# Order of TensorE's three kinds of attention products inside one core step of a two-layer macaron block

## Chip, cores and metric

The program runs on one core of a Trainium2 chip. The metric is the device time of one execution in microseconds (us), the median of several runs.

## The reference

The input is 8 sequences of 1024 tokens with 256 features. Six residual sublayers follow each other, each on a layernorm of the residual: a gated feed-forward block, linear attention (16 heads, chunks of 64), the gated block again, a routed low-rank layer, causal softmax attention, and the routed layer again. The softmax attention is what the change touches:

```
q = q * cos + rotate_half(q) * sin
k = k * cos + rotate_half(k) * sin
scores = jnp.einsum('bhqd,bhkd->bhqk', q, k) * scale
scores = jnp.where(causal, -jnp.inf, scores)
attn = jax.nn.softmax(scores, axis=-1)
out = jnp.einsum('bhqk,bhkd->bhqd', attn, v)
```

The kernel takes it over 1024 tokens and 16 heads of 16 features for each of the 8 sequences.

## The kernel before

**Three streams.** The work of each engine is a list of pieces, one list for each *tick* of a fixed plan (`weave`). The *front* generators bring a sequence (two halves of 512 tokens, `c` = 0 and 1) through the first sublayers up to rotated q and k, which go to DRAM. The *core* is the softmax attention, in steps; the *tail* generators do the output product and the last sublayer. Fronts and tails of other sequences run in the same ticks as the core, and fill the engines beside it. Within a tick the order is: part 0 of the core step, front `c` = 0, part 1, front `c` = 1, part 2, tails. A table (`STEPS`) says how many core steps a tick has, mostly one.

**The core.** A group is 4 heads of one sequence; there are 32 groups. A group takes two passes.

- *First pass*: `score(g, i)` multiplies q by k for a 128-query block (one to two matmuls, up to 512 columns in all) into one of two PSUM banks. VectorE takes the row maximum of each (line 1115 for blocks with the causal diagonal, line 1118 for the others), and adds 1 to the semaphore `r_used` when it has read a bank. The two banks are a ring, `r_take`: product number n waits until number n-2 has been read. Two kinds of transposes go through the same ring: that of the maxima (line 818, one a group) and that of the sums of values (line 812, two a group). VectorE runs its core pieces one tick later than TensorE.
- *Second pass*: `tscore(u)` multiplies k by q, for one key block and two heads: two matmuls of 128 to 512 columns, into banks 0 and 1. ScalarE takes the exponential of each (line 1321). There is one bank for each of the two heads, so the product for unit u, half j, waits until the exponential of unit u-1, half j, has been read (`exp_done`). GpSimd zeroes what lies above the diagonal (line 1469).
- *Values*: `values(u)`, every second step, multiplies four heads' exponentials by v (line 795); it waits for the exponentials and for GpSimd.

A core step t has the transposed products of unit u+1 (u = t - 129) in part 0, the values in part 1 when u is even, and up to three first-pass products of the group that is 30 steps ahead, one in each part, as the table `USES` says: mostly one in a step with values and two in a step without. A sequence has 96 steps and 144 first-pass products.

A semaphore wait stands in TensorE's own queue, and matmuls leave it in the order of the program. The lines that the change reorders are in `core_pe`.

Of the kernel before, what the change touches and what calls it, by code (L numbers as in the profile page):

```python
# [18 lines left out]
NB = B  # L19
# [37 lines left out]
def macaron(nc, a, out):  # L57
    ctx = ExitStack()
    with ctx:
# [105 lines left out]
        def ps(i, n=1):  # L165
            return bank[i // 2][:, (i % 2) * CH:(i % 2) * CH + n * CH]
# [213 lines left out]
        NU = NTU * NG  # L380
# [14 lines left out]
        score_at = {}  # L395
# [18 lines left out]
        def width(c, kb):  # L414
            return CH - max(0, kb - 4 * c) * P

        def slot(g, hp):
            return (2 * g + hp) % NSLOT

        def loads(g, hp):  # L420

            return (2 * g + hp) // NSLOT + 1
# [11 lines left out]
        if True:  # L434

            with nc.Block() as block:
# [22 lines left out]
                def r_take(*key):  # L459
                    n = len(rtab)  # L460
                    rtab[key] = n
                    if n >= 2:
                        nc.tensor.wait_ge(s["r_used"], n - 1)
                    return ps(3 + n % 2)
# [289 lines left out]
                def score(g, i):  # L754

                    h, blocks = sunits[i]
                    b_ = slot(g, h // 2)
                    nc.tensor.wait_ge(stack_in[b_], 16 * ND * loads(g, h // 2))
                    bk = r_take("s", g, i)
                    for qb, k0, n, col in blocks:  # L760
                        last = mm(bk[:, col:col + n], stq[b_][:, h % 2, qb * P:(qb + 1) * P], stk[b_][:, h % 2, k0:k0 + n],  # L761
                                  start=True, stop=True)
                    last.then_inc(s["r_full"], 1)

                def tscore(u):

                    g, i = divmod(u, NTU)
                    c, kb, hp = tunits[i]
                    if i == 0:
                        nc.tensor.wait_ge(max_in[g % 2], 64 * (g // 2 + 1))  # L770
                    n = width(c, kb)
                    b_ = slot(g, hp)
                    for j in range(2):
                        if u >= 1:
                            nc.tensor.wait_ge(s["exp_done"], 2 * u + j - 1)
                        mm(ps(j)[:, 0:n], stk[b_][:, j, kb * P:(kb + 1) * P],  # L776
                                  stq[b_][:, j, (c + 1) * CH - n:(c + 1) * CH], start=True, stop=True).then_inc(
                                      s["t_ps"], 1)

                def values(u):  # L780

                    g, i = divmod(u, NTU)
                    c, kb, _ = tunits[i]
                    yu = NC * g + c
                    n = width(c, kb)
                    if g % NG == 0 and kb % 4 == 0:
                        nc.tensor.wait_ge(s["v_in"], 32 * (g // NG) + 16 * (kb // 4 + 1))
                    nc.tensor.wait_ge(s["exp_done"], 2 * u + 2)
                    if i in DIAG:
                        nc.tensor.wait_ge(s["causal"], len(DIAG) * g + DIAG.index(i) + 1)  # L790
                    if kb == 0 and yu >= 1:
                        nc.tensor.wait_ge(s["ypv_done"], yu)
                    for j in range(G):
                        at = VP * (G * (g % NG) + j)
                        last = mm(ps(2)[HP * j:HP * (j + 1), CH - n:CH], vsm[:, kb, at:at + HP], pexp[:, (u - 1 + j // 2) % NPX, j % 2, 0:n],  # L795
                                  start=kb == 0, stop=kb == 4 * c + 3, tile_position=(0, HP * j))
                    last.then_inc(s["pv_done"], 1)

                def core_pe(t, part):
                    u = t - SX  # L800
                    if part == 0 and 0 <= u + 1 < NU * NB:
                        tscore(u + 1)
                    if part == 1 and u % 2 == 0 and 2 <= u < NU * NB + 1:
                        values(u - 1)
                    if (t, part) in score_at:
                        score(*score_at[t, part])
                    if part == 2 and t in y_tr_at:
                        g, c = y_tr_at[t]
                        nc.tensor.wait_ge(s["ypv_done"], NC * g + c + 1)
                        bk = r_take("y", g, c)  # L810
                        for k in range(4):
                            last = nc.tensor.transpose(bk[:, k * P:(k + 1) * P], ypv[:, c, k * P:(k + 1) * P], ident[:])
                        last.then_inc(s["r_full"], 1)
                    if part == 2 and t in max_tr_at:
                        g = max_tr_at[t]
                        nc.tensor.wait_ge(s["mx_comb"], g + 1)
                        bk = r_take("m", g)
                        nc.tensor.transpose(bk[0:G * NT, 0:P], mxa[:, g % 2], ident[:]).then_inc(s["r_full"], 1)

                @block.tensor  # L820
                def _(pe):
                    weave(core_pe, front_pe, tail_pe)
# [792 lines left out]
```

## Time and profile before

| | |
|---|---|
| median of 3 runs | 2871.23 us (2869.66 to 2884.01) |
| profiled execution, its own time | 2874.38 us |
| its span, first to last instruction | 2872.6 us |
| TensorE (PE) | 2595.6 us busy, 90% |
| VectorE (DVE) | 1856.1 us, 65% |
| ScalarE (ACT) | 1227.1 us, 43% |
| GpSimd (POOL) | 746.5 us, 26% |

Busy time is the union of the records of an engine. A matmul's record reaches from its start to the end of its pipeline, so that records of matmuls that follow each other overlap. PEld are the weight loads of TensorE.

### The profile page before, as it was taken

Reading aid. Unit: us, or ns where it says so; the run is one execution under the profiler, and the core shown is the slowest. Engines: PE = TensorE matmul, PEld = TensorE weight load, DVE = VectorE, ACT = ScalarE, POOL = GpSimd, SP = SyncE. Lnnn points to the kernel's source line nnn. Section 1 sums busy time; section 2 is a strip of 40 time slices with the busy share of each in tenths; the row PEclk is TensorE's granted clock in tenths of the full one; section 3 lists DMA queues with packets and bytes.
Section 4 is the critical chain, followed back from the end, with each engine's and each line's share of the span. In section 5 each row is a group of like instructions: output and inputs, shape, how many; then the busy total and the mean of one; then the engine's idle time right before and its main releaser. Section 6 shows DMA issues by size and latency. Waiting matters only on the chain.

```text
span 2872.6 us, 45484 instructions
## 1 busy us (share of the span) xinstructions
PE 2595.6 (90%) x15278; PEld 1723.4 (60%) x15278; DVE 1856.1 (65%) x5534; ACT 1227.1 (43%) x2802; POOL 746.5 (26%) x1283
## 2 busy tenths in 40 slices
PE   3885899989999999999999999999999999998996
PEld 3563566556666666566655666566665666555644
DVE  5543667766677667776677766676677766776642
ACT  1321244455444444444444444444444444444452
POOL 2322222223322232223322232222322233221111
PEclk7987899999899999999999999999999999999997
DMA  2014112321244112322044112341124221343311
GB/s 61 1 45 120 22 41 62 109 60 40 48 108 110 40 42 62 116 71 65 18 113 125 42 34 61 95 110 40 42 62 131 63 58 30 97 123 74 75 36 48
DMA packets 137423, 193.97 MB, mean 68 GB/s; under 512 B 49439, under 2 KB 111214, under 8 KB 127854
## 3 DMA queue, kind: packets, MB, share of 16 engines
q1 hardware_dynamic: 131808, 190.89, 26.3%
q8 instruction: 129, 2.11, 0.3%
q10 hardware_dynamic: 5390, 0.18, 0.1%
q14 instruction: 96, 0.79, 0.1%
HBM read 122.34 MB, written 67.63 MB: 66 GB/s over the span
## 4 chain that ended last, share of the span: by engine, by line
PE 69%; DVE 16%; DMA 8%; issue 2%; POOL 2%; ACT 1%; SPq 1%; DVEq 0%; ACTq 0%; POOLq 0%
PE bank L776 9%; PE bank L795 8%; PE bank L761 8%; DMA arena<-rope_table 6%; PE bank L598 5%; PE bank L578 4%; PE bank L547 4%; PE bank L529 4%; DVE bank L1115 4%; PE bank L538 3%; PE bank L689 3%; PE bank L703 3%; PE bank L633 2%; PE bank L508 2%; PE bank L572 2%
## 5 line engine op out<-in xcount | busy, mean ns | idle before, releaser
L1321 ACT ACTIVATE pexp<-bank 128x512 f32<-128x512 f32 (+3 forms) x1536 | 677.3, 498 | 571.6 <-PE bank L776 571.1
L1115 DVE CUSTOM_DVE_ANT_0 bank<-bank,maskneg 128x256 f32<-128x256 f32 (+3 forms) x1024 | 484.7, 511 | 266.0 <-PE bank L761 262.0
L776 PE MATMUL bank<-stq,stk 128*128 128x512 f32 (+3 forms) x1536 | 548.6, 427 | 28.9 <-ACT pexp L1321 23.6
L761 PE MATMUL bank<-stk,stq 128*128 128x512 f32 (+3 forms) x1536 | 505.3, 393 | 68.3 <-DVE mxa L1115 24.0
L776 PEld LDWEIGHTS bank<-stq,stk 128*128 128x128 f32 x1536 | 267.9, 195 | 315.4 <-ACT pexp L1321 190.5
L1118 DVE TENSOR_REDUCE mxa<-bank 128x1 f32<-128x512 f32 x512 | 346.3, 684 | 144.7 <-PE bank L761 140.3
L1469 POOL TENSOR_SCALAR_AFFINE_SELECT pexp<-pexp 128x256 f32<-128x256 f32 x512 | 213.2, 424 | 753.7 <-ACT pexp L1321 753.6
L761 PEld LDWEIGHTS bank<-stk,stq 128*128 128x128 f32 x1536 | 281.2, 197 | 180.6 <-issue 142.0
L795 PE MATMUL bank<-pexp,vsm 128*32 128x512 f32 (+3 forms) x3072 | 342.4, 519 | 20.1 <-POOL pexp L1469 19.9
L1387 POOL TENSOR_SCALAR_AFFINE_SELECT arena<-arena 128x512 f32<-128x512 f32 x128 | 78.6, 639 | 404.4 <-ACT arena L1223 404.4
L598 PE MATMUL bank<-arena 32*128 32x256 f32 x1024 | 153.7, 419 | 8.0 <-DVE arena L922 5.0
L508 PE MATMUL bank<-ident,arena 128*128 128x128 f32 x768 | 117.0, 300 | 47.0 <-DVE arena L839 42.3
L922 DVE TENSOR_TENSOR arena<-bank,mask 128x512 f32<-128x512 f32 x128 | 82.4, 685 | 92.6 <-PE bank L598 92.6
L529 PE MATMUL bank<-arena,wk 128*128 128x256 f32 x512 | 137.2, 419 | 4.7 <-DVE arena L863 4.5
L508 PEld LDWEIGHTS bank<-ident,arena 128*128 128x128 f32 x768 | 100.0, 156 | 65.7 <-DVE arena L839 47.9
L795 PEld LDWEIGHTS bank<-pexp,vsm 128*32 128x32 f32 x3072 | 62.6, 110 | 123.4 <-issue 95.2
L1140 ACT COPY xnT<-bank 128x512 f32<-128x512 f32 x160 | 88.3, 601 | 107.5 <-PE bank L508 107.2
L1338 POOL TENSOR_SCALAR varep<-mv 128x4 f32<-128x4 f32 x96 | 22.6, 235 | 417.6 <-DVE mv L833 417.1
L598 PEld LDWEIGHTS bank<-arena 32*128 32x128 f32 x1024 | 92.5, 194 | 57.2 <-issue 39.9
L529 PEld LDWEIGHTS bank<-arena,wk 128*128 128x128 f32 x512 | 107.8, 214 | 28.9 <-issue 6.1
L538 PE MATMUL bank<-wr,arena 128*128 128x256 f32 x512 | 122.9, 383 | 0.1
L839 DVE TENSOR_SCALAR arena<-x,mv,rstd 128x256 f32<-128x256 f32 x320 | 114.8, 420 | 12.0 <-POOL rstd L1340 11.3
(186 smaller groups left out, 4058.4 us busy)
## 6 DMA issues: line engine op xcount, KB each, us to landing
stq<-q_halves SPq DMA_DIRECT2D x128, 256.0 KB
arena<-rope_table SPq DMA_DIRECT2D x8, 2048.0 KB
q_halves<-arena SPq DMA_DIRECT2D x32, 512.0 KB, 2.8
k_halves<-arena SPq DMA_DIRECT2D x32, 512.0 KB, 2.9
stk<-k_halves SPq DMA_DIRECT2D x64, 256.0 KB
stk<-k_halves SPq DMA_DIRECT2D x128, 128.0 KB
v_rows<-arena SPq DMA_DIRECT2D x16, 544.0 KB, 4.1
vsm<-v_rows SPq DMA_DIRECT2D x16, 544.0 KB, 3.7
```

What stands on the lines that cost most here:

```text
L508: last = nc.tensor.transpose(bk[:, t * P:(t + 1) * P], src[:, t, k * P:(k + 1) * P], ident[:])
L529: last = mm(bk[:, m * D:(m + 1) * D], wk0[:, k, m * P:(m + 1) * P], xmA[:, h, k], start=k == 0, stop=k == KT - 1)
L538: last = mm(bk[:, i * D:(i + 1) * D], xmB[:, p, k, i * P:(i + 1) * P], wr0[:, k], start=k == 0, stop=k == KT - 1)
L547: last = mm(bk[:, i * D:(i + 1) * D], kact[:, p, k, i * P:(i + 1) * P], wv0[:, k], start=k == 0, stop=k == KT - 1)
L598: last = mm(bks[i][:, k * D:(k + 1) * D], khT[rows, k, j * P:(j + 1) * P], qbd[rows, j % 2, k], start=k == 0, stop=k == KT - 1, skip_group ...
L761: last = mm(bk[:, col:col + n], stq[b_][:, h % 2, qb * P:(qb + 1) * P], stk[b_][:, h % 2, k0:k0 + n], start=True, stop=True)
L776: mm(ps(j)[:, 0:n], stk[b_][:, j, kb * P:(kb + 1) * P], stq[b_][:, j, (c + 1) * CH - n:(c + 1) * CH], start=True, stop=True).then_inc(s["t ...
L795: last = mm(ps(2)[HP * j:HP * (j + 1), CH - n:CH], vsm[:, kb, at:at + HP], pexp[:, (u - 1 + j // 2) % NPX, j % 2, 0:n], start=kb == 0, sto ...
L1115: last = nc.vector.tensor_tensor_reduce(out=sc, in0=sc, in1=maskneg[:, CH - n:CH], scale=1.0, scalar=LOWEST, op0=ALU.add, op1=ALU.max, acc ...
L1118: last = nc.vector.reduce_max(dst, sc, AX)
L1321: nc.scalar.activation(pexp[:, u % NPX, j, 0:n], ps(j)[:, 0:n], ACT.Exp, scale=DK ** -0.5).then_inc(s["exp_done"], 1)
L1469: nc.gpsimd.affine_select(out=v, in_=v, compare_op=ALU.is_ge, fill=0.0, base=0, pattern=[[0, 2], [1, P]], channel_multiplier=-1).then_inc( ...
```

## The change

In each core step's part 0 the first-pass product, if there is one, now stands ahead of the transposed products; in part 1 it stands ahead of the values. In part 2 nothing changes, nor on any other engine. The front and tail pieces stand where they stood, between the parts.

```diff
                 def core_pe(t, part):
                     u = t - SX
+                    if (t, part) in score_at:
+                        score(*score_at[t, part])
+                    if part == 1 and u % 2 == 0 and 2 <= u < NU * NB + 1:
+                        values(u - 1)
                     if part == 0 and 0 <= u + 1 < NU * NB:
                         tscore(u + 1)
-                    if part == 1 and u % 2 == 0 and 2 <= u < NU * NB + 1:
-                        values(u - 1)
-                    if (t, part) in score_at:
-                        score(*score_at[t, part])
                     if part == 2 and t in y_tr_at:
```

TensorE's queue at units 434 and 435, before. Line 776 is `tscore`, line 761 `score`, line 795 `values`; in brackets stand the semaphores that the instruction waits for (`stack` is the load of q and k).

```order
L776 MATMUL bank<-stq,stk 128x384 [waits exp_done] x2
L761 MATMUL bank<-stk,stq 128x512 [waits r_used,stack3]
L761 MATMUL bank<-stk,stq 128x256 [waits r_used,stack3]
L761 MATMUL bank<-stk,stq 128x256
L776 MATMUL bank<-stq,stk 128x384 [waits exp_done] x2
L761 MATMUL bank<-stk,stq 128x512 [waits r_used,stack3]
L795 MATMUL bank<-pexp,vsm 32x512 [waits ypv_done,causal,exp_done]
L795 MATMUL bank<-pexp,vsm 32x512 x3
```

The same place after the change, from the transposed products of unit 434 on.

```order
L776 MATMUL bank<-stq,stk 128x384 [waits exp_done] x2
L761 MATMUL bank<-stk,stq 128x256 [waits r_used,stack3]
L761 MATMUL bank<-stk,stq 128x256
L761 MATMUL bank<-stk,stq 128x512 [waits r_used,stack3]
L776 MATMUL bank<-stq,stk 128x384 [waits exp_done] x2
L795 MATMUL bank<-pexp,vsm 32x512 [waits ypv_done,causal,exp_done]
L795 MATMUL bank<-pexp,vsm 32x512 x3
```

The 512-column first-pass product of the second step has changed places with the pair of transposed products that was ahead of it. (The one of the first step has done so too; it now stands above the rows shown.)

TensorE's queue at unit 395, before:

```order
L776 MATMUL bank<-stq,stk 128x512 [waits exp_done] x2
L761 MATMUL bank<-stk,stq 128x512 [waits r_used,stack0]
L795 MATMUL bank<-pexp,vsm 32x512 [waits ypv_done,exp_done,v_in]
L795 MATMUL bank<-pexp,vsm 32x512 x3
L598 MATMUL bank<-arena 128x256 [waits f_free2,qbd1,f_free0,f_free1]
```

and after:

```order
L761 MATMUL bank<-stk,stq 128x512 [waits r_used,stack0] x2
L776 MATMUL bank<-stq,stk 128x512 [waits exp_done] x2
L795 MATMUL bank<-pexp,vsm 32x512 [waits ypv_done,exp_done,v_in]
L795 MATMUL bank<-pexp,vsm 32x512 x3
L598 MATMUL bank<-arena 128x256 [waits f_free2,qbd1,f_free0,f_free1]
```

The first of the two merged rows on line 761 is the second product of the step before; the other has moved ahead of the transposed pair. The values and the front's product (line 598) stand where they did.

## Rows read from the trace of the kernel before

**Rows 1.** The page: span, TensorE's busy time, granted clock in 40 slices.

```profile
span 2872.6 us, 45484 instructions
PE 2595.6 (90%) x15278; PEld 1723.4 (60%) x15278; DVE 1856.1 (65%) x5534; ACT 1227.1 (43%) x2802; POOL 746.5 (26%) x1283
PEclk7987899999899999999999999999999999999997
```

**Rows 2.** Busy time in the stretch where the core runs beside fronts.

```profile
core 0: us, PE busy (x) PEld busy (x) DVE busy (x) ACT busy (x) POOL busy (x), PEclk, DMA share, GB/s
370.00:2500.00 2130.00, 2018.04 (x12207) 1344.39 (x12206) 1449.04 (x4346) 974.97 (x2234) 582.72 (x998) 0.97 0.28 69
```

**Rows 3.** Waits, whole span: who waited for whom: us, times, longest.

```profile
ACT pexp L1321 <- PE bank L776: 571.1, 433, 6.5
...
DVE bank L1115 <- PE bank L761: 262.0, 219, 7.5
...
DVE mxa L1118 <- PE bank L761: 140.3, 115, 3.8
```

**Rows 4.** TensorE's own waits, whole span, same columns.

```profile
PE bank L761 <- DVE mxa L1115: 24.0, 28, 3.1
PE bank L776 <- ACT pexp L1321: 23.6, 35, 1.3
...
PE bank L761 <- DVE mxb L1115: 23.5, 40, 1.7
...
PE bank L818 <- DVE mxa L1115: 18.9, 17, 1.3
...
PE bank L761 <- DVE mxa L1118: 11.1, 20, 1.0
...
PE bank L812 <- DVE mxb L1115: 7.1, 9, 1.3
...
PE bank L812 <- DVE mxa L1118: 4.3, 5, 1.8
```

**Rows 5.** Timeline, TensorE, nothing waited for: start us, us, what.

```profile
1499.88 0.63 PE L776 MATMUL bank<-stq,stk 128*128 128x512 f32 x2
1500.35 0.40 PE L761 MATMUL bank<-stk,stq 128*128 128x512 f32 x1
1500.68 0.64 PE L795 MATMUL bank<-pexp,vsm 128*32 128x512 f32 x4
```

**Rows 6.** Timeline at units 434 and 435; in brackets idle before, releaser.

```profile
1857.78 0.69 DVE L1017 SCALAR_TENSOR_TENSOR x<-bank,x 128x512 f32<-128x512 f32 x1 [2.27 <-PE bank L690]
1857.93 0.63 PE L761 MATMUL bank<-stk,stq 128*128 128x512 f32 x3
...
1858.56 0.83 PE L776 MATMUL bank<-stq,stk 128*128 128x384 f32 x2
1858.56 1.41 DVE L830 BATCH_NORM_STATS2 stats<-x 128x6 f32<-128x256 f32 x4
...
1860.30 0.67 DVE L1115 CUSTOM_DVE_ANT_0 bank<-bank,maskneg 128x512 f32<-128x512 f32 x1
...
1861.18 0.47 PE L761 MATMUL bank<-stk,stq 128*128 128x512 f32 x1 [1.79 <-DVE mxa L1115]
```

**Rows 7.** Timeline, TensorE, other first products of a step that waited.

```profile
1605.39 0.47 PE L761 MATMUL bank<-stk,stq 128*128 128x512 f32 x1
...
1645.23 0.99 PE L776 MATMUL bank<-stq,stk 128*128 128x512 f32 x2
...
1646.05 0.45 PE L761 MATMUL bank<-stk,stq 128*128 128x512 f32 x1
...
1717.53 0.47 PE L761 MATMUL bank<-stk,stq 128*128 128x512 f32 x1 [0.52 <-DVE mxb L1115]
...
1775.17 0.52 PE L761 MATMUL bank<-stk,stq 128*128 128x128 f32 x2 [0.91 <-DVE mxa L1118]
...
1843.35 0.47 PE L761 MATMUL bank<-stk,stq 128*128 128x512 f32 x1 [0.26 <-DVE mxb L1115]
...
1895.87 0.47 PE L761 MATMUL bank<-stk,stq 128*128 128x512 f32 x1
```

**Rows 8.** Timeline, TensorE, transposed products that waited for ScalarE.

```profile
1643.76 0.99 PE L776 MATMUL bank<-stq,stk 128*128 128x512 f32 x2 [0.79 <-ACT pexp L1321]
...
1888.21 0.98 PE L776 MATMUL bank<-stq,stk 128*128 128x512 f32 x2 [0.63 <-ACT pexp L1321]
```

**Rows 9.** Timeline, a transpose behind a VectorE run that a first product began.

```profile
1784.53 0.30 DVE L1115 CUSTOM_DVE_ANT_0 bank<-bank,maskneg 128x128 f32<-128x128 f32 x1 [1.49 <-PE bank L761]
...
1785.55 0.63 PE L812 MATMUL bank<-ident,ypv 128*128 128x128 f32 x4 [0.71 <-DVE mxb L1115]
```

## Prediction

> **What bounds the kernel now.** I read the page first. TensorE is busy for 90% of the span, more than any other engine, and its clock is granted at nine tenths or more in most slices [rows 1]. Start and end have little core work, so the next view is the stretch from 370 to 2500 us. There TensorE has a record running in 2018.04 of 2130 us, so it stands still for 112 us in all, 5%, and the granted clock is 0.97, which is the upper of the two levels nearly throughout [rows 2]. No reordering can win more than about those 112 us and what the ends hold, and one that lets TensorE stand still longer pays for it almost in full.
>
> Then the waits. VectorE waits for first-pass products for 262.0 and 140.3 us and ScalarE waits for transposed ones for 571.1 us [rows 3]: both have room, and both stand idle at most places until TensorE delivers. The other way round the waits are short. TensorE's first-pass products wait for a bank that VectorE has still to read, 24.0 + 23.5 + 11.1 = 58.6 us in 88 places; its transposed products wait for ScalarE for 23.6 us in 35 places; the transposes of maxima and sums, which take from the same two banks, wait 18.9 and 7.1 + 4.3 us in 17 and 14 places [rows 4]. These four are what the change can move.
>
> **The change.** Nothing is added or removed. Call S0 the first-pass product of part 0, S1 that of part 1, T the transposed pair, V the values. Before, a step was T S0 (front) V S1 (front); now it is S0 T (front) S1 V (front). With one product in a step with V and two in the next, TensorE's core work read T S0 V T S0 S1, and now reads S0 T V S0 T S1. Distances from one T to the next, and from one S0 to the next, stay the same as long as both have a product between them. So a plain shift costs nothing: where TensorE waits for VectorE because VectorE itself had waited for an S0, both move together by one T, and the wait stays as it is. The same holds for T and ScalarE. What counts are waits whose cause did not move with them: a run of VectorE or ScalarE work that began at a front product, or at S1.
>
> *Size of the pieces.* With nothing waited for, T of 512 columns starts at 1499.88, the S0 behind it at 1500.35 and V at 1500.68 [rows 5]. So a wide pair takes 0.47 us of TensorE, and one product of 512 columns half of that, 0.23 us. The group's pairs have 384 columns on average, 0.35 us; behind a wait a product's record is 0.47 long and not 0.40 [rows 5, 6], so I take 0.43 us for a pair that starts behind a wait.
>
> *Loss 1: T is no longer done while S0 waits.* The clearest place is at units 434 and 435. VectorE is held by a front piece (it got its input from line 690, not from a first-pass product), does its statistics from 1858.56, and starts on the score maxima at 1860.30. TensorE does T at 1858.56 and then stands for 1.79 us until S0 can start at 1861.18 [rows 6]. The bank comes free at the same time whatever TensorE did, so with S0 ahead of T, T and V follow after 1861.18, and TensorE leaves this place one pair later. A place like this costs the smaller of the wait (counted from where T started) and the pair. Between 1563 and 1898 us, one sequence's 96 steps, I find eleven S0 that start at the moment in which their bank is released, the first at 1605.39 and the last at 1895.87; four of them show an idle engine (0.52, 0.91, 0.26 and 1.79 us), in the others T filled the wait, as at 1645.23, where S0 starts 0.82 us after T and not 0.47 [rows 6, 7]. In three of the eleven VectorE's run had begun with an S0: no loss. The eight that are left have two behind each other in one unbroken VectorE run, around 1843, which counts once. Seven places by 0.43 are 3.0 us a sequence. There are eight sequences, the last without fronts beside part of its core, so 7.5: **+23 us**. Bounds: nothing, if each VectorE run moved with the products; and all 88 waits by 0.47, 41 us.
>
> *Loss 2: T starts later, and so does its exponential.* A step has T behind S0 now, 0.23 us later, and behind S0's wait. Where the next step has a product of its own this is the plain shift. Some 8 of 96 steps have none; about 21 of those in the whole run wait for the exponential today, by my reading, and each then waits 0.23 us longer: 5 us. What a T that was held at one of loss 1's places adds at the next T I put at 3 us, since at most of them ScalarE has more than a microsecond to spare. **+8 us**. V waits for the same exponentials but stands a whole T behind them, and gets nothing.
>
> *Gain 1: S0 fills waits of T.* At 1643.76 and 1888.21 T stands 0.79 and 0.63 us until ScalarE, which was busy with front copies, has read the bank [rows 8]. If S0's bank is free by then, S0 now goes into that hole. It is 35 visible places by 0.23 [rows 4]: **-8 us** (bounds: nothing, and the whole 23.6).
>
> *Gain 2: VectorE gets S0 one T earlier.* At 1784.53 VectorE has waited 1.49 us for an S0, and the transpose of sums that needs the bank behind it then waits 0.71 us until 1785.55 [rows 9]. S0 comes one T earlier, and the transpose with it. The transposes wait in 17 + 14 places; in about 22 of them VectorE's run begins with an S0: 22 by 0.43 is 9, and S1 products with the same cause give 3 more. **-12 us**. The first T of a group, which waits for the maxima to come back by DMA, gives perhaps -2.
>
> *Sum.* 23 + 8 - 8 - 12 - 2 = +9 us. On the profiled execution's own 2874.38 that is 2883; against the median of 2871.23 it is **2880 us**, 0.3% slower. The difference between the two sizes of before, 3 us, is the usual one between a profiled and a timed run, and I keep it out.
>
> **Rivals.** By this kernel's spread a measurement tells 0.5%, 14 us, from no change; the forecast lies inside it.
>
> *A: nearly nothing happens.* Each delay of T is taken up by the next place where TensorE would have waited anyway, since waits end at a time set by the fronts. For it: loss 1's places are a few microseconds in front of others. Against it: 95% busy leaves only 112 us of waits to hide in [rows 2]. Time: 2871 to 2875. The Trainium skill has a rule that would make this likelier: its page Perfetto Trace Analysis, section Identifying the Most-Contended Engine, says that matmul busy time is a bad measure of how near TensorE is to its limit, and that the busy share of weight loads is a better one. Here that share is 1344.39 of 2130, 63% [rows 2]. By the page over a third would be room, and the sum would be near 0; by the rows TensorE's start-to-start times at a place without waits (0.23 us a product) leave no room, and the sum stands. I hold with the rows and give A its chance.
>
> *B: slower by over 0.5%.* One mechanism: the wait of S0 now holds T, T holds the exponential, and ScalarE, which is in order, then holds its front copies behind it. The 571.1 us that ScalarE waits for T [rows 3] are waits in its queue's order, and the front's pieces stand behind them. Then each of the S0 waits costs the pair and again a part of it in the fronts: 41 us of pairs from the bound of loss 1, less the 22 us of gains, and 15 to 20 more in the fronts gives 2905. It decides from the point where a held T makes the next T or a front product wait. Against it: ScalarE is busy for only 974.97 of 2130 us [rows 2].
>
> *C: faster by over 0.5%.* VectorE's 402 us of waits for products shrink, its whole schedule moves ahead by up to 0.43 us a step, and the score waits shrink with it, whatever began the run. Then the 88 + 17 + 14 places of [rows 4] each lose some 0.3 us, 36 us, with gain 1 on top and loss 1 gone: 2871 - 44 + 8 = 2835; half of it is 2853. It decides at whether VectorE's runs in front of TensorE's waits begin with an S0. Against it: at 1857.78 the run began with the front [rows 6], and so did those at seven of eleven places.
>
> **How the numbers follow.** The forecast and A together, all within 0.5%: 0.48 (A alone 0.15). B: 0.36. C: 0.16. Slower has more than faster since the loss is read at named places with long waits, the gains at short ones. The range takes in B's time but for its tail, and C's half: 2852 to 2906.
>
> **What the profile of the changed kernel would show.** TensorE's products of line 761 wait more for VectorE: 58.6 becomes 75 to 85 us. Those of line 776 wait less for ScalarE: 23.6 becomes about 15. Line 818 and 812's 30.3 us become about 20. At the place of [rows 6], the pair and the values stand behind the S0, which starts when it did relative to the statistics on VectorE. VectorE's 402 us of waits for line 761 should hardly change, or fall a little. ScalarE's waits for line 776 should not fall. If line 761's waits fall instead, loss 1 is wrong and C holds; if line 776's waits for ScalarE grow, or the front products' waits do, B holds.

## The result, and the profile after

The changed kernel took 2904.36 us (median of 4 runs, 2895.76 to 2912.58) against 2870.44 us, a ratio of 1.0104 with a 95% interval of 1.0081 to 1.0127. So it is 1.0% slower, some 30 us (23 to 36). The forecast was 2880 us and "within 0.5%". The time lies inside the range (2852 to 2906) by less than 2 us, outside the case held likeliest, and beside the 2905 us of rival B.

The page of the changed kernel: span, busy times, granted clock, and three groups of products (busy us, mean ns, idle before, releaser).

```profile
span 2900.2 us, 45484 instructions
...
PE 2579.5 (89%) x15278; PEld 1721.7 (59%) x15278; DVE 1851.2 (64%) x5534; ACT 1231.6 (42%) x2802; POOL 752.0 (26%) x1283
...
PEclk8996899999999999999999999999999999999998
...
L761 PE MATMUL bank<-stk,stq 128*128 128x512 f32 (+3 forms) x1536 | 612.9, 444 | 141.6 <-DVE mxb L1115 57.2
...
L776 PE MATMUL bank<-stq,stk 128*128 128x512 f32 (+3 forms) x1536 | 452.0, 373 | 14.6 <-ACT pexp L1321 12.8
...
L795 PE MATMUL bank<-pexp,vsm 128*32 128x512 f32 (+3 forms) x3072 | 351.1, 531 | 14.6 <-POOL pexp L1469 13.3
```

Its TensorE waits, in the columns of [rows 4]:

```profile
PE bank L761 <- DVE mxb L1115: 57.2, 51, 3.0
PE bank L508 <- DVE arena L839: 41.7, 10, 11.5
PE bank L761 <- DVE mxa L1115: 37.5, 41, 3.1
PE bank L761 <- DVE mxa L1118: 30.5, 35, 2.0
...
PE bank L818 <- DVE mxa L1115: 17.1, 17, 1.5
...
PE bank L776 <- ACT pexp L1321: 12.8, 36, 0.6
...
PE bank L812 <- DVE mxb L1115: 5.2, 9, 1.3
...
PE bank L812 <- DVE mxa L1118: 2.5, 4, 1.8
```

The first-pass products' waits for VectorE went from 58.6 to 125.2 us, those of the transposed products for ScalarE from 23.6 to 12.8, those of the two transposes from 30.3 to 24.8. TensorE stands still for 320.7 us of the span (2900.2 - 2579.5), where it was 277.0 (2872.6 - 2595.6). The values' waits for GpSimd (L795) fell from 19.9 to 13.3 us. These four changes, 66.6 - 10.8 - 5.5 - 6.6, add up to the 43.7 us by which the standing grew; the others are small and about cancel. The span grew by 27.6 us only, since TensorE's busy time fell by 16.1: a pair that used to run by itself inside a wait now overlaps the products around it, as in the rows below.

The same place as [rows 6] in the changed kernel:

```profile
1875.64 0.69 DVE L1017 SCALAR_TENSOR_TENSOR x<-bank,x 128x512 f32<-128x512 f32 x1 [2.42 <-PE bank L690]
...
1876.42 1.40 DVE L830 BATCH_NORM_STATS2 stats<-x 128x6 f32<-128x256 f32 x4
...
1879.03 0.47 PE L761 MATMUL bank<-stk,stq 128*128 128x512 f32 x1 [2.61 <-DVE mxa L1115]
...
1879.34 0.51 PE L776 MATMUL bank<-stq,stk 128*128 128x384 f32 x2
...
1879.79 1.89 PE L795 MATMUL bank<-pexp,vsm 128*32 128x512 f32 x8
```

From VectorE's statistics to the first-pass product it is 2.61 us, and it was 2.62 (1858.56 to 1861.18). At this place TensorE's order does not move the release. The pair, which used to run at the start of that time, now starts 0.31 us after its end.

### The profile page after: what moved, and what is told of

Read it like the earlier page. It is cut to its first block, busy times and chain, and to the rows that moved or that the text cites. A ratio compares the mean times of both kernels' runs of the same rounds, so it can differ in the third digit from the quotient of the medians.

```text
span 2900.2 us, 45484 instructions
## 1 busy us (share of the span) xinstructions
PE 2579.5 (89%) x15278; PEld 1721.7 (59%) x15278; DVE 1851.2 (64%) x5534; ACT 1231.6 (42%) x2802; POOL 752.0 (26%) x1283
## 4 chain that ended last, share of the span: by engine, by line
PE 68%; DVE 16%; DMA 8%; issue 3%; POOL 1%; SPq 1%; ACT 1%; DVEq 0%; ACTq 0%; POOLq 0%
PE bank L761 9%; PE bank L795 9%; PE bank L776 7%; DMA arena<-rope_table 7%; PE bank L598 5%; DVE bank L1115 4%; PE bank L578 4%; PE bank L547 4%; PE bank L538 3%; PE bank L529 3%; PE bank L703 3%; PE bank L689 3%; PE bank L633 2%; PE bank L572 2%; PE bank L644 2%
## 5 line engine op out<-in xcount | busy, mean ns | idle before, releaser
L1321 ACT ACTIVATE pexp<-bank 128x512 f32<-128x512 f32 (+3 forms) x1536 | 674.3, 495 | 667.4 <-PE bank L776 665.6
L761 PE MATMUL bank<-stk,stq 128*128 128x512 f32 (+3 forms) x1536 | 612.9, 444 | 141.6 <-DVE mxb L1115 57.2
L776 PE MATMUL bank<-stq,stk 128*128 128x512 f32 (+3 forms) x1536 | 452.0, 373 | 14.6 <-ACT pexp L1321 12.8
L1469 POOL TENSOR_SCALAR_AFFINE_SELECT pexp<-pexp 128x256 f32<-128x256 f32 x512 | 219.2, 433 | 797.6 <-ACT pexp L1321 797.6
L795 PE MATMUL bank<-pexp,vsm 128*32 128x512 f32 (+3 forms) x3072 | 351.1, 531 | 14.6 <-POOL pexp L1469 13.3
L776 PEld LDWEIGHTS bank<-stq,stk 128*128 128x128 f32 x1536 | 298.2, 199 | 103.2 <-ACT pexp L1321 56.2
L508 PE MATMUL bank<-ident,arena 128*128 128x128 f32 x768 | 119.2, 304 | 46.3 <-DVE arena L839 41.7
L795 PEld LDWEIGHTS bank<-pexp,vsm 128*32 128x32 f32 x3072 | 62.9, 110 | 118.0 <-issue 92.8
L547 PE MATMUL bank<-wv,arena 128*128 128x256 f32 x512 | 122.3, 382 | 0.1
```

What stands on the lines that cost most here:

```text
L508: last = nc.tensor.transpose(bk[:, t * P:(t + 1) * P], src[:, t, k * P:(k + 1) * P], ident[:])
L547: last = mm(bk[:, i * D:(i + 1) * D], kact[:, p, k, i * P:(i + 1) * P], wv0[:, k], start=k == 0, stop=k == KT - 1)
L776: mm(ps(j)[:, 0:n], stk[b_][:, j, kb * P:(kb + 1) * P], stq[b_][:, j, (c + 1) * CH - n:(c + 1) * CH], start=True, stop=True).then_inc(s["t ...
L1321: nc.scalar.activation(pexp[:, u % NPX, j, 0:n], ps(j)[:, 0:n], ACT.Exp, scale=DK ** -0.5).then_inc(s["exp_done"], 1)
L1469: nc.gpsimd.affine_select(out=v, in_=v, compare_op=ALU.is_ge, fill=0.0, base=0, pattern=[[0, 2], [1, P]], channel_multiplier=-1).then_inc( ...
```

## Experiments

Each kernel was timed in 5 rounds beside the kernel before on the same chip; differences in us are the ratio's times the median of before, with the interval's ends in brackets. *S0*, *S1*, *T* and *V* are the first-pass product of part 0, that of part 1, the transposed pair and the values. **Theory W**: what stands ahead of a waiting product in TensorE's queue is free, what stands behind it comes later. **Rival X**: a later T makes its exponential and what hangs on it late. **Rival Y**: the values are what costs. **Rival Z**, of the last experiments, stands in their expectation.

### The two halves of the change

```diff
+                    if part == 0 and (t, part) in score_at:
+                        score(*score_at[t, part])
                     if part == 0 and 0 <= u + 1 < NU * NB:
                         tscore(u + 1)
                     if part == 1 and u % 2 == 0 and 2 <= u < NU * NB + 1:
                         values(u - 1)
-                    if (t, part) in score_at:
+                    if part and (t, part) in score_at:
```

> Only the first-pass product of part 0 (S0) stands ahead of the transposed pair (T); part 1 is as before. Theory W (the pair used to run while S0 waited for VectorE, and now stands behind that wait): all of the loss is here, +28 to +36 us, and line 761 waits for VectorE for about 125 us where it was 58.6. Rival Y (the values, now behind S1, are what costs): under +8 us.

Measured: 2897.65 us, ratio 1.0066 (1.0044 to 1.0088), +19 us (13 to 25). Line 761's waits for VectorE are 125.4 us (57.2, 37.2 and 31.0), as W said, but the time is less than W's 28.

The other half, S1 ahead of V only:

```diff
                     if part == 0 and 0 <= u + 1 < NU * NB:
                         tscore(u + 1)
+                    if part == 1 and (t, part) in score_at:
+                        score(*score_at[t, part])
                     if part == 1 and u % 2 == 0 and 2 <= u < NU * NB + 1:
                         values(u - 1)
-                    if (t, part) in score_at:
+                    if part != 1 and (t, part) in score_at:
```

> Only the first-pass product of part 1 stands ahead of the values; part 0 is as before. It touches 61 of the 384 steps with values. Theory W: within 4 us of before, line 761 waits about 60 us. Rival Y: +20 us or more.

Measured: 2889.68 us, ratio 1.0042 (1.0023 to 1.0061), +12 us (7 to 18). Both readings missed: it is not nothing, and not all. The two halves add up to 31 us, the whole change within its interval.

### Which steps: part 1

S1 ahead of V in a chosen set of steps, `(t - SX + LEAD) % NU` being the step's number among a sequence's 96:

```diff
+                    ahead = part == 1 and (t - SX + LEAD) % NU in (26, 60, 90)
                     if part == 0 and 0 <= u + 1 < NU * NB:
                         tscore(u + 1)
+                    if ahead and (t, part) in score_at:
+                        score(*score_at[t, part])
                     if part == 1 and u % 2 == 0 and 2 <= u < NU * NB + 1:
                         values(u - 1)
-                    if (t, part) in score_at:
+                    if not ahead and (t, part) in score_at:
```

> S1 ahead of the values only in steps 26, 60 and 90 of a sequence, those in which the trace of before shows S1's bank not yet free when the values start. Theory W: the whole loss of the part 1 change, +8 to +15 us. Rival (the values, and with them the release of the exponentials' buffers, are later): three eighths of it, +4 us.

Measured: 2898.35 us, ratio 1.0071 (1.0048 to 1.0093), +20 us (14 to 27): more than W's 15.

> S1 ahead of the values only in the other five such steps (2, 10, 36, 46, 86), where S1's bank is free when the values start. Theory W: within 4 us of before. Rival (later values): +7 us.

Measured (the same edit with steps 2, 10, 36, 46, 86): 2876.28 us, ratio 0.9995 (0.9977 to 1.0013), -1 us (-7 to 4). So the loss of part 1 sits in the three steps in which S1 waits for its bank. The three steps cost no less than all eight; the intervals overlap, and the mean granted clock was lower with the three (0.942 in the runs, against 0.945 with all eight). In the profile of the three-step kernel TensorE stands for 9.5 us more than before (286.5 us), and is busy for 14.6 us more (2610.2 us). Step 60 in the kernel before: statistics of VectorE, pair, values, S1.

```profile
1798.68 0.52 PE L776 MATMUL bank<-stq,stk 128*128 128x128 f32 x2
...
1799.19 1.41 DVE L830 BATCH_NORM_STATS2 stats<-x 128x6 f32<-128x256 f32 x4 [1.39 <-DMA arena<-rope_table]
1799.46 0.64 PE L795 MATMUL bank<-pexp,vsm 128*32 128x256 f32 x8
...
1801.80 0.47 PE L761 MATMUL bank<-stk,stq 128*128 128x512 f32 x1 [1.70 <-DVE mxb L1115]
```

and in the changed one:

```profile
1816.85 1.40 DVE L830 BATCH_NORM_STATS2 stats<-x 128x6 f32<-128x256 f32 x4 [1.49 <-DMA arena<-rope_table]
...
1819.47 0.47 PE L761 MATMUL bank<-stk,stq 128*128 128x512 f32 x1 [2.19 <-DVE mxb L1115]
1819.86 0.42 PE L795 MATMUL bank<-pexp,vsm 128*32 128x256 f32 x4
```

From the statistics to S1 it is 2.61 and 2.62 us. VectorE is itself held by a DMA here, that of the rotation table (1.39 and 1.49 us). The values used to run in that time, and now stand behind it.

### Which steps: part 0

The same kind of edit with `part == 0`, and three sets of steps. S0 goes ahead of T

```diff
+                    ahead = part == 0 and (t - SX + LEAD) % NU in (6, 12, 20, 23, 40, 54, 64, 68, 71, 72, 74, 75, 76, 80, 82, 87, 88, 94)
+                    if ahead and (t, part) in score_at:
+                        score(*score_at[t, part])
                     if part == 0 and 0 <= u + 1 < NU * NB:
                         tscore(u + 1)
...
-                    if (t, part) in score_at:
+                    if not ahead and (t, part) in score_at:
```

> S0 stands ahead of T only in 18 of a sequence's 96 steps, those in which the trace of before shows S0's bank not yet free when T starts (6, 12, 20, 23, 40, 54, 64, 68, 71, 72, 74, 75, 76, 80, 82, 87, 88, 94). Theory W: the whole loss sits here, +28 to +40 us. Rival X (T is later in every step): about 18/96 of the loss, +6 us.

Measured: 2899.37 us, ratio 1.0078 (1.0058 to 1.0098), +22 us (17 to 28). 18 of 96 steps hold all that part 0 loses. X's 6 us lie outside the interval. So do all but the lower end of W's 28 to 40 us: W priced the steps too high.

> S0 stands ahead of T in all steps but the 18 in which its bank was not yet free. Theory W: what is left are the filled waits of T, 0 to 12 us faster than before. Rival X: most of the loss is here, +20 us or more.

Measured (`not in` the same set): 2874.49 us, ratio 0.9992 (0.9978 to 1.0007), -2 us (-6 to 2). In 78 steps of 96 a T that stands behind S0 costs nothing, and X falls for them. For the other 18, where T is held longer, the waits speak against it: in the kernel with S0 ahead in those, T waits 11.5 us for ScalarE where it was 23.6, and the values 14.0 us for GpSimd where it was 19.9.

> S0 stands ahead of T only in nine of a sequence's 96 steps (13, 14, 19, 21, 39, 58, 73, 86, 90), those in which the trace of before shows T waiting for ScalarE with S0's bank free. Theory W: S0 fills the wait, at most 0.23 us a place, so 5 to 12 us faster than before. Rival X (a later T costs): no change or slower.

Measured (`in (13, 14, 19, 21, 39, 58, 73, 86, 90)`): 2874.69 us, ratio 0.9996 (0.9982 to 1.0011), -1 us (-5 to 3). The gain of 5 to 12 us is not there: T's waits for ScalarE fell by 2.0 us only, from 23.6 to 21.6, and line 761's for VectorE rose from 58.6 to 66.9. The waits of the kernel with S0 ahead in the 78 steps show a loss of the same kind:

```profile
PE bank L776 <- ACT pexp L1324: 31.6, 74, 1.5
PE bank L761 <- DVE mxb L1118: 27.2, 38, 2.1
PE bank L761 <- DVE mxa L1118: 26.5, 34, 3.1
...
PE bank L821 <- DVE mxa L1118: 17.0, 17, 1.5
```

(Its line numbers from the edit on are higher by 3: 821 is the transpose of the maxima.) T's waits for ScalarE did not fall from 23.6 us, they rose to 31.6, in 74 places and not 35. My reading, which no run tests, is that T is later, so its exponential is, and the next T waits for it.

The waits of the kernel with S0 ahead in the 18 steps:

```profile
PE bank L761 <- DVE mxb L1118: 53.4, 52, 2.7
...
PE bank L761 <- DVE mxa L1118: 41.0, 44, 3.1
PE bank L761 <- DVE mxa L1121: 30.1, 33, 1.9
```

They add up to 124.5 us, nearly the 125.2 of the whole change.

### VectorE's reads made short

Both kernels here leave out most of the row maxima: each block is read in 64 columns only. Lines cut out of the edit:

```diff
-                            sc = r_bank("s", g, i)[:, col:col + n]
+                            r = 64
+                            sc = r_bank("s", g, i)[:, col + n - P:col + n - P + r]
...
-                                last = nc.vector.tensor_tensor_reduce(out=sc, in0=sc, in1=maskneg[:, CH - n:CH], scale=1.0, scalar=LOWEST,
+                                last = nc.vector.tensor_tensor_reduce(out=sc, in0=sc, in1=maskneg[:, CH - P:CH - P + r], scale=1.0, scalar=LOWEST,
...
-                            nc.scalar.activation(pexp[:, u % NPX, j, 0:n], ps(j)[:, 0:n], ACT.Exp, scale=DK ** -0.5).then_inc(s["exp_done"], 1)
+                            nc.scalar.activation(pexp[:, u % NPX, j, 0:n], ps(j)[:, 0:n], ACT.Exp, scale=1e-6).then_inc(s["exp_done"], 1)
```

> The order of before, but VectorE reads 64 columns of each first-pass block and not all of it (so the row maxima are those of 64 keys only, and the exponentials are taken at a scale of 1e-6 to stay finite; both leave the timing of everything else as it is). A bank is read in some 0.2 us and not 0.7. Both theories: TensorE's waits for VectorE on line 761 fall from 58.6 to under 15 us, and the kernel is 30 to 70 us faster than before.

Measured: 2819.51 us, ratio 0.9791 (0.9768 to 0.9815), -60 us (-67 to -53).

> The changed order with the same short reads of 64 columns (row maxima of 64 keys only, exponentials at a scale of 1e-6). Theory W: without waits for the banks the order costs nothing, so this is within 6 us of the short-read kernel with the order of before. Rival X (T and its exponential are simply later, and ScalarE's and the fronts' work behind them): still 20 us or more slower than that one.

Measured: 2825.17 us, ratio 0.9820 (0.9794 to 0.9846), -52 us (-59 to -44). The two medians are 5.7 us apart, inside W's 6 and outside X's 20, but with intervals of 7 us to either side that does not tell the two well, and the runs do not do what they were made for. The waits of the first, then of the second:

```profile
PE bank L761 <- DVE mxb L1116: 21.5, 12, 3.2
...
PE bank L761 <- DVE mxa L1116: 14.9, 14, 2.1
...
PE bank L761 <- DVE mxa L1119: 3.3, 8, 0.8
```

```profile
PE bank L761 <- DVE mxb L1116: 52.4, 33, 5.4
...
PE bank L761 <- DVE mxa L1116: 21.8, 17, 2.1
...
PE bank L761 <- DVE mxa L1119: 17.1, 25, 1.1
```

39.7 us of waits are left with the old order, where both theories said under 15, and 91.3 with the new one. So the length of VectorE's reads is not all that holds the banks; [rows 6] show front pieces ahead of them in its queue at one place; that they do the rest everywhere is not shown. As a test of W against X I take it as inconclusive; the sets of steps decide.

### The other way round: more work ahead of the waiting product

If what stands ahead of a waiting S0 is free, V belongs there too.

```diff
+                    early = (t - SX + LEAD) % NU in (12, 40, 54, 64, 74, 76, 80, 88)
                     if part == 0 and 0 <= u + 1 < NU * NB:
                         tscore(u + 1)
-                    if part == 1 and u % 2 == 0 and 2 <= u < NU * NB + 1:
+                    if part == (0 if early else 1) and u % 2 == 0 and 2 <= u < NU * NB + 1:
                         values(u - 1)
```

> The order of before, but in eight of a sequence's 96 steps (12, 40, 54, 64, 74, 76, 80, 88) the values stand right behind the transposed pair, ahead of S0: the steps in which S0 waits for its bank even behind the pair. Theory W (what stands ahead of a waiting product is free): the values, up to 1 us, go into that wait; the idle time in front of these S0 adds up to some 40 us, of which 20 to 30 can be filled, so 12 to 28 us faster than before. Rival Z (VectorE's chain is what counts there; the product comes later to VectorE and the wait comes back at the next one): within 6 us of before.

Measured: 2871.82 us, ratio 0.9976 (0.9959 to 0.9993), -7 us (-12 to -2), short of W's 12; by its size it could be Z, which allowed 6.

```profile
PE bank L795 <- POOL pexp L1470: 32.3, 21, 2.7
PE bank L761 <- DVE mxb L1116: 24.1, 18, 3.0
```

The score waits fell to 46.8 us, but the values' waits for GpSimd's mask rose from 19.9 to 32.3. At step 54 the wait moved from S0 to the values: over the eight sequences TensorE stands in front of the values there for 15.2 us where it was 5.1, and in front of S0 for nothing where it was 6.3.

> The values stand right behind the transposed pair, ahead of S0 and of the front piece, in all 384 steps with values. Theory W: fills the same waits as the eight steps, but where GpSimd has not finished the mask the values now wait themselves (19.9 us of such waits before): between 15 us faster and 10 us slower. Rival Z: 10 us slower or more.

Measured (`early = True`): 2912.32 us, ratio 1.0116 (1.0092 to 1.0139), +33 us (26 to 40). W is out here and Z's "10 us slower or more" is met; the values' waits for GpSimd are 44.2 us there. So the one order does not suit every step.

> The order of before, with the values ahead of S0 in six of 96 steps (40, 64, 74, 76, 80, 88): the eight without 12 and 54. At 54 the trace of the eight-step kernel shows S0's wait gone and the values waiting for GpSimd in its place. Theory W: the two steps left out gained nothing, so this is as fast as the eight-step kernel or a little faster, 5 to 12 us faster than before. Rival Z: within 3 us of before.

Measured (steps 40, 64, 74, 76, 80, 88): 2858.49 us, ratio 0.9932 (0.9913 to 0.9951), -20 us (-25 to -14). It is faster than the kernel before and than the changed one, and beyond the 12 us expected. Its page and its waits:

```profile
span 2859.4 us, 45484 instructions
...
PE 2577.6 (90%) x15278; PEld 1713.1 (60%) x15278; DVE 1856.3 (65%) x5534; ACT 1227.4 (43%) x2802; POOL 746.4 (26%) x1283
...
PE bank L508 <- DVE arena L840: 47.8, 16, 11.5
...
PE bank L795 <- POOL pexp L1470: 20.3, 21, 2.4
...
PE bank L761 <- DVE mxb L1116: 17.1, 18, 2.2
PE bank L761 <- DVE mxa L1116: 16.5, 28, 3.1
...
PE bank L761 <- DVE mxa L1119: 11.8, 20, 1.0
...
PE bank L776 <- DMA stq<-mlo: 9.3, 9, 2.6
```

The score waits are down to 45.4 us, and the values' are back at 20.3. But TensorE does not stand still for less than before: 281.8 us (2859.4 - 2577.6) against 277.0. What the score waits lost came back elsewhere, as in the front's line 508 (42.3 before) and in T's wait for the maxima by DMA (1.8 before). The whole gain of this execution, 13.2 us of span, is in TensorE's busy time, 2577.6 against 2595.6 us, at a mean granted clock of 0.953 against 0.946. So this run shows that the order gains, and not that it gains by filling waits; the last section has the clock. The place of [rows 6] in it:

```profile
1846.66 0.82 PE L776 MATMUL bank<-stq,stk 128*128 128x384 f32 x2
1846.67 1.41 DVE L831 BATCH_NORM_STATS2 stats<-x 128x6 f32<-128x256 f32 x4
1847.61 1.06 PE L795 MATMUL bank<-pexp,vsm 128*32 128x512 f32 x8
...
1849.29 0.47 PE L761 MATMUL bank<-stk,stq 128*128 128x512 f32 x1 [0.61 <-DVE mxa L1116]
```

Once more S0 starts 2.62 us after the statistics, with pair and values inside: three orders, one release at this place.

## Why the prediction was half right

- *Bound, and which waits matter*: right. TensorE's standing still grew by 43.7 us of the span and the time by 28 (profiled executions, 2874.38 and 2901.96). The four waits that the prediction named all moved the way it said.
- *Loss 1*, the pair behind S0's wait, 23 us at seven places a sequence: the 18 steps cost 22 us (17 to 28). The mechanism is where it was said to be, but that the sum agrees is in part luck. There are 18 steps in which S0's bank is not yet free when T starts, where I had found eleven such products and counted seven, so a step cost far less than the 0.43 us that I gave it (22 us over 18 steps of eight sequences is 0.15 us), and by the estimate of the last section some 10 of the 22 us go with the clock, which loss 1 does not have. The profile's check on it failed: I expected line 761 to wait 75 to 85 us and it was 125.2. I had sized the growth by what is lost, but the idle record also shows the pair that used to stand in the wait and is done afterwards.
- *Loss 2 and gains 1 and 2*, together -14 us with the DMA's 2: failed. The 78 other steps hold -2 us (-6 to 2). In the run with those steps gain 2 shows as 5.6 us less waiting at the transposes of maxima and of sums (30.3 before; 17.0, 5.2 and 2.5 in it), not 12, and gain 1 is outweighed, T's waits for ScalarE rising by 8.0 us. I had priced T's later start only at the eight steps without a product. In the nine steps' own trace T's waits fell by 2.0 us and line 761's rose by 8.3; why, is not shown.
- *Part 1* was the step left out: I wrote that the values "get nothing" from the move, and did not look at S1's waits with the values ahead of them. It costs 12 us (7 to 18), in the three steps where S1 waits, so it is a place of the same kind as those of loss 1, with the values as the work that covered the wait.
- *The clock* was put at nothing, without a reason: the prediction read 0.97 in the core and went on. The mean granted clock fell from 0.946 to 0.941 in the profiled executions, which by the same estimate is some 12 of the 30 us.
- *The sum*: 22 - 2 + 12 = 32 us by the runs, 30 measured; mine was 23 - 14 + 0 = 9. (The clock is inside the 22 and not a further term.)
- *Rival A* is out: its 2871 to 2875 us leave at most 5 us of loss, and the interval begins at 23. With it goes the reading by weight loads that the prediction took from the Trainium skill (Perfetto Trace Analysis, section Identifying the Most-Contended Engine): their busy share of 60% left no room that took up the waits. *Rival B* has the time by luck, not by its mechanism: ScalarE's wait for line 776 did grow, from 571.1 to 665.6 us, but T's own waits for ScalarE fell to 12.8, and the front's waits stayed, those of line 508 at 42.3 and 41.7. *Rival C* is out: VectorE's waits for line 761 did shrink, from 402.3 to 379.6 us, and the score waits grew.
- What the values' move gained was partly given back at step 60, where VectorE waits for the DMA of the rotation table. In the trace of the eight-step kernel TensorE stands for 16.8 us in front of S1 at this step, over the eight sequences, and it was 7.4; VectorE's statistics wait for that DMA for 16.4 us in the whole run, and it was 7.4. No run tests it.

## What to carry to other kernels

In an in-order queue the price of a swap is paid at the places where one of the two waits, so list those places one by one, for every pair that changes order, and ask of each what released it. Here the loss sat in those places: 22 us in 18 of a sequence's 96 steps and -2 in the other 78, 20 us in three steps with values and -1 in five others. Values moved ahead of the waiting product in six of the 96 steps gained 20 us; the same move wherever there are values lost 33 us. Then look at TensorE's clock as well as at its waits: the six-step kernel is faster without standing still for less. A sum of waits is no measure of time: 67 us more of them were 30 us.

## What had not been expected of the hardware

TensorE's clock takes part. After the stand of 2.61 us in the changed kernel the values took 1.89 us, where the six-step kernel's take 1.06. Granted clock in three stretches of the changed kernel (columns of [rows 2]: PEclk is the third number from the end), the last after that stand:

```profile
1734.90:1736.50 1.60, 1.53 (x11) 0.64 (x11) 1.60 (x2) 0.73 (x2) 1.60 (x3) 1.00 0.00 0
1736.50:1743.30 6.80, 6.80 (x22) 4.59 (x19) 4.59 (x8) 1.44 (x3) 0.75 (x1) 0.50 0.01 2
1879.90:1883.30 3.40, 3.40 (x14) 1.56 (x13) 2.46 (x9) 1.23 (x4) 0.58 (x2) 0.50 0.00 0
```

The level is 1.00, and 0.50 for 6.8 us though TensorE is busy throughout, after it had stood for 3.03 us up to 1734.97. In the six-step kernel it is 1.00 at the same place:

```profile
1848.50:1852.00 3.50, 1.93 (x11) 1.02 (x7) 3.50 (x12) 0.66 (x2) 2.43 (x5) 1.00 0.18 63
```

The kernel before falls to the lower level at these two places as well (after stands of 1.25 and 0.52 us, and of 1.79 us), so it is a matter of how much of the time. With only the levels 1.0 and 0.5 a mean of 0.946 is 10.8% of the span at the lower one, 310 us; the changed kernel's 0.941 is 342 us and the six-step kernel's 0.953 is 269 us. Half of 32 us is 16, the most that the clock can have added to the 27.6 between these two executions.

Runs of one and the same program give an estimate. The kernel before was timed 73 times beside the experiments, at 2866 to 2890 us and a mean clock of 0.951 to 0.941; in a straight line through these runs 0.001 less of the clock goes with 2.0 us more. By that price, with the mean clocks of all timed runs of a kernel and of the runs of before beside them:

| kernel | clock, and that of before | measured | of it with the clock (estimate) |
|---|---|---|---|
| the change | 0.940, 0.946 | +30 us | 12 |
| S0 ahead in 18 steps | 0.941, 0.946 | +22 us | 10 |
| S1 ahead of the values | 0.945, 0.946 | +12 us | 1 |
| S1 ahead in three steps | 0.942, 0.946 | +20 us | 8 |
| values early, all steps | 0.946, 0.946 | +33 us | 1 |
| values early, eight steps | 0.952, 0.946 | -7 us | -11 |
| values early, six steps | 0.953, 0.947 | -20 us | -12 |

(For the change only the profiled execution of before has its clock on record.) So part 1 as a whole and the values early everywhere lose nearly by the order alone, and in the change and in the six-step kernel the clock has a large share. It stays an estimate: in these runs clock and time only go together, and no run held the clock and moved the order.
